# Where batches 1 to 7 and the later weights are prepared: all ahead, or between the pairs of batches 0 and 1

## What is computed

```python
xn = _layernorm(x, axis=-1)
x = x + _L0_attn_ref(xn, ...) + _L0_ffn_ref(xn, ...)
# _L0_attn_ref, 16 heads of 64
q = (x @ Wq + bq).reshape(b, s, H, L)
k = (x @ Wk + bk).reshape(b, s, H, L)
v = (x @ Wv + bv).reshape(b, s, H, L)
q = _apply_rope(q, cos, sin)
k = _apply_rope(k, cos, sin)
scores = jnp.where(causal, scores, -1000000000.0)
attn = jax.nn.softmax(scores, axis=-1)
return attended @ Wo + bo
# _L0_ffn_ref
x_scale = jnp.maximum(jnp.abs(x2).max() / 127.0, EPS)
x_int8 = jnp.clip(jnp.round(x2 / x_scale), -128, 127).astype(jnp.int8)
```

## Time and profile before

| | us |
| --- | --- |
| median of 3 executions | 1175.89 |
| lowest and highest | 1175.56 and 1179.27 |
| the profiled execution, as timed | 1179.43 |
| its span in the trace | 1177.6 |
| PE, DVE, ACT, POOL busy | 1029.2, 891.5, 690.7, 766.0 |
| span until VectorE's last row maximum | 100.4 |
| phases ahead of the pairs, until turn 0 on VectorE | 146.4 |
| second layer, after the last pair's `av` | 233 |

### The profile page before, as it was taken

How to read it: one execution, slowest core, us unless ns; L and a number is a source line. 1 busy time by engine, 2 the same in 40 slices (tenths; PEclk the granted TensorE clock), 3 DMA queues, 4 the chain that set the end, 5 groups by cost and what they waited for, 6 DMA issues and landing times.

```text
span 1177.6 us, 23657 instructions
## 1 busy us (share of the span) xinstructions
PE 1029.2 (87%) x7944; PEld 667.5 (57%) x7944; DVE 891.5 (76%) x1869; ACT 690.7 (59%) x1831; POOL 766.0 (65%) x949
## 2 busy tenths in 40 slices
PE   2005699999999999999999999999999965899988
PEld 1002265666766766666676676666667742454444
DVE  7695567777777777777777777777777637999996
ACT  1252276666666666666666666666667604766764
POOL 0081586777877687787777778677776515756662
PEclk9999899999999999999999999999999986999999
DMA  9303423233233223223323422332322000010001
GB/s 330 98 0 113 147 95 112 82 121 104 82 116 94 87 91 128 89 86 113 99 82 101 125 82 94 108 95 86 111 93 82 1 1 1 1 36 18 18 27 45
DMA packets 99693, 100.02 MB, mean 85 GB/s; under 512 B 12928, under 2 KB 94848, under 8 KB 99200
## 3 DMA queue, kind: packets, MB, share of 16 engines
q1 hardware_dynamic: 99584, 98.63, 25.8%
HBM read 56.64 MB, written 41.94 MB: 84 GB/s over the span
## 4 chain that ended last, share of the span: by engine, by line
PE 73%; DVE 17%; issue 3%; DMA 3%; ACT 1%; SPq 1%; DVEq 1%; POOL 0%; ACTq 0%; POOLq 0%
PE bank L1270 25%; PE bank L1358 13%; PE bank L1344 12%; PE bank L1373 7%; PE bank L1331 6%; PE bank L1332 5%; DVE arena L1181 3%; PE bank L1333 2%; DMA x_sb<-in_x 2%; DVE nm L1151 1%; PE bank L1520 1%; DVE wmax L952 1%; DVE arena L918 1%; DVE arena L1200 1%; DVE arena L1165 1%
## 5 line engine op out<-in xcount | busy, mean ns | idle before, releaser
L529 POOL TENSOR_SCALAR arena<-arena,rc 128x128 f32<-128x128 f32 (+3 forms) x512 | 274.9, 555 | 196.6 <-DVE rc L1031 196.6
L699 ACT ACTIVATE arena<-bank,nm 128x256 f32<-128x256 f32 (+3 forms) x512 | 268.0, 526 | 84.1 <-DVE nm L1023 75.2
L1023 DVE TENSOR_REDUCE nm<-bank 128x1 f32<-128x256 f32 (+3 forms) x512 | 230.0, 481 | 108.7 <-PE bank L1333 105.1
L1344 PE MATMUL bank<-ident,arena 128*128 128x128 f32 x1280 | 216.5, 277 | 4.8 <-DVE arena L1038 4.4
L1344 PEld LDWEIGHTS bank<-ident,arena 128*128 128x128 f32 x1280 | 143.7, 141 | 41.2 <-DVE arena L1038 20.3
L707 ACT ACTIVATE arena<-bank 128x512 f32<-128x512 f32 (+3 forms) x256 | 111.2, 434 | 80.0 <-PE bank L1344 79.8
L1332 PE MATMUL bank<-arena 128*128 128x256 f16 (+3 forms) x512 | 153.6, 300 | 0.0
L1358 PE MATMUL bank<-arena 128*64 128x512 f32 (+3 forms) x1024 | 151.9, 439 | 0.0
L1331 PE MATMUL bank<-arena 128*128 128x256 f16 (+3 forms) x512 | 147.8, 302 | 2.3 <-ACT arena L699 2.3
L1038 DVE COPY arena<-bank 128x512 f32<-128x512 f32 (+3 forms) x256 | 124.2, 485 | 23.8 <-PE bank L1344 19.9
L1358 PEld LDWEIGHTS bank<-arena 128*64 128x64 f32 x1024 | 67.8, 136 | 94.3 <-issue 71.3
(11 more groups left out here) (148 smaller groups left out, 2226.8 us busy)
## 6 DMA issues: line engine op xcount, KB each, us to landing
arena<-scr SPq DMA_DIRECT2D x320, 128.0 KB, 2.5
scr<-arena SPq DMA_DIRECT2D x256, 128.0 KB, 1.7
x_sb<-in_x SPq DMA_DIRECT2D x8, 512.0 KB, 6.4
arena<-in_weights SPq DMA_DIRECT2D x2, 2048.0 KB, 13.8
out<-x_sb SPq DMA_DIRECT2D x16, 256.0 KB, 2.2
xscr<-xsh SPq DMA_DIRECT2D x8, 256.0 KB, 2.3
xscr<-xsl SPq DMA_DIRECT2D x8, 256.0 KB, 2.2
xsh<-xscr SPq DMA_DIRECT2D x8, 256.0 KB, 3.2
```

The source lines that it names most:

```text
L529: last = pool.tensor_scalar(pr[slot][:, OFF[i]:OFF[i + 1]], pr[slot][:, OFF[i]:OFF[i + 1]], rc[:, slot, i:i + 1], 1.0, ALU.mult, ALU.mult)
L699: act.activation(pr[slot][:, OFF[i]:OFF[i + 1]], s_tile[i], ACT.Exp, bias=nm[:, slot, i:i + 1], accum_out=sm[:, slot, i:i + 1]).then_inc(e ...
L1023: dve.tensor_reduce(nm[:, slot, i:i + 1], s_tile[i], AX.X, ALU.max, negate=True).then_inc(max_done, 1)
L1344: last = pe.transpose(banks[5 + h][:, (i - j) * P:(i - j + 1) * P], pr[2 * par + h][:, OFF[i] + j * P:OFF[i] + (j + 1) * P], ident[:])
```

## The change

`wst`, `xn1` and the tables no longer have room of their own: they lie over the buffers of attention pieces and outputs that are not yet in use (`wst_qk` over `pr`, `tabraw` and `w8st` over `ptf`, `xn1` over `oth` and `otl`). The opening now does batch 0's rows and the query and key weights alone. GpSimd, not VectorE, writes the normal rows and the rotation tables; VectorE, not GpSimd, takes the low parts of the weights. VectorE's `early(n)` stands at the end of its turn n and holds the rest in portions; TensorE's `columns_of_rows(n, k)`, ScalarE's `columns_high` and VectorE's `columns_low` stand inside turns 1 to 7, and for turns 0 to 7 the copies of head 1's pieces 0 and 2 go from VectorE to ScalarE. The one reduction of the weights' maxima becomes four (query and key; values in turn -3; output weights in turn 3; second layer's in turn 10), and that of the rows' maxima comes in turn 6. The five first phases use two PSUM banks in turn (`o_bank`) instead of one, the first layer's steps of quantising batch 0 all come in turn 7, and the statistics write `mv3` without a copy.

```diff
+            load_rows(0)
+            for k in range(KT):
+                half = slice(k * C_V // KT, (k + 1) * C_V // KT)
+                sp.dma_start(wst_qk[:, half], weights_d[:, half]).then_inc(wqk_loaded, 16)
+            sp.dma_start(tabraw[:], tab_d).then_inc(tab_loaded, 16)
...
+            def normal_rows(b):
+
+                pool.wait_ge(roots_done, {0: 1, 1: 2, 2: 2, 3: 2}.get(b, 3))
+                after(pool, amax_done, b - 1)
+                after(pool, xt1_done, KT * (b - 1))
+                for c in range(NT):
+                    t = b * NT + c
+                    last = pool.tensor_scalar(xn1[b % 2][:, c, :], x_sb[:, t, :], mv3[:, t, 0:1], nw3[:, 0, t:t + 1],
+                                              ALU.subtract, ALU.mult)
+                last.then_inc(xn1_done, 1)
+
+            def weight_maxima(groups):
+
+                pool.wait_ge(wmax_done, groups.stop)
+                pool.partition_all_reduce(wall[:, groups], wmax[:, groups], P, bass.bass_isa.ReduceOp.absmax).then_inc(wall_done, 1)
+
+            normal_rows(0)
+            weight_maxima(slice(G_Q, G_V))
+            pool.wait_ge(setup_done, 1)
+            pool.wait_ge(tab_loaded, 16)
+            for g, by, dsts in ((G_Q, L ** -0.5, (cosq, sinq)), (G_K, 1.0, (cosk, sink))):
+                for a, dst in enumerate(dsts):
+                    last = pool.tensor_scalar(dst[:], tabraw[:, a], sc[:, g:g + 1], by, ALU.mult, ALU.mult)
+                last.then_inc(tab_done, 1)
...
+                if n == 1 - AHEAD + 1:
+                    weight_maxima(slice(G_V, G_O))
+                if 0 <= n < NB - 1:
+                    normal_rows(n + 1)
+                if n == 3:
+                    weight_maxima(slice(G_O, G_L))
+                if n == NB - 2:
+                    pool.wait_ge(xm_done, 1)
+                    pool.partition_all_reduce(xmax[:], xmax1[:], P, bass.bass_isa.ReduceOp.absmax).then_inc(xall_done, 1)
+                if n == 10:
+                    weight_maxima(slice(G_L, NG))
...
+            def later_weights(n):
+
+                if n == 2 - AHEAD:
+                    act.wait_ge(c_loaded, 16 * 4)
+                    act.activation(w8[:], w8st.rearrange("p (k c w) -> p k c w", k=KT, w=2)[:, :, :, 0], ACT.Copy).then_inc(w8_done, 1)
+                elif n == 3 - AHEAD:
+                    act.wait_ge(setup_done, 2)
+                    weights_high(G_V, wv_hi)
+                elif n == 4 - AHEAD:
+                    act.wait_ge(rows_mm, 1)
+                    for t in range(2):
+                        act.activation(fbow[:, t], ob[:, 0:D], ACT.Copy)
+                        last = act.activation(wsxw[:, t], ob[:, D:2 * D], ACT.Copy)
+                    last.then_inc(fb_done, 1)
+                elif n == 5:
+                    act.wait_ge(setup_done, 3)
+                    weights_high(G_O, wo_hi)
+                elif 12 <= n < 12 + NG - G_L:
+                    act.wait_ge(setup_done, 4)
+                    weights_high(G_L + n - 12, wr_hi)
...
+                if 1 <= n < NB:
+                    columns_high(n, 0)
+                if shared_copies(n):
+                    pt_whole(n, 0, 1)
...
+            row_sums(0)
+            inverse_roots(slice(0, 1), 0)
+            dve.wait_ge(wqk_loaded, 32)
+            weight_maximum(slice(G_Q, G_V))
             for k in range(KT):
-                dve.tensor_scalar(diag[:, k], ident[:], fbo[:, k:k + 1], None, ALU.mult)
-                last = dve.tensor_scalar(diag[:, KT + k], ident[:], vec[:, V_FS + k:V_FS + k + 1], None, ALU.mult)
-            last.then_inc(diag_done, 1)
-            dve.tensor_tensor(sc_vo[:], sc[:, G_V:G_V + 1], sc[:, G_O:G_O + 1], ALU.mult)
-            dve.scalar_tensor_tensor(out=sc_c[:], in0=sc[:, G_L:G_L + 1], scalar=D ** -0.5, in1=sc[:, G_R:G_R + 1],
-                                     op0=ALU.mult, op1=ALU.mult)
-            link(dset, dve.tensor_tensor(thr_c[:], inv[:, G_L:G_L + 1], inv[:, G_R:G_R + 1], ALU.mult))
-            dve.scalar_tensor_tensor(out=thr_c[:], in0=thr_c[:], scalar=D ** 0.5, in1=thr[:], op0=ALU.mult, op1=ALU.mult)
-            dve.tensor_scalar(sc_hr[:], sc[:, G_WR:G_WR + 1], 0.5, None, ALU.mult)
-            dve.tensor_scalar(sc_hv[:], sc[:, G_WV:G_WV + 1], 0.5, None, ALU.mult)
-            dve.tensor_scalar(omu[:], vec[:, V_MUR:V_MUR + 4], -1.0, 1.0, ALU.mult, ALU.add)
-            rows_of(1)
-            dve.wait_ge(amax_done, NB)
-            dve.tensor_reduce(xmax1[:], amax[:], AX.X, ALU.max).then_inc(xm_done, 1)
+                columns_low(0, k)
+            weight_scale(slice(G_Q, G_V), 0)
+            dve.wait_ge(b_loaded, 16 * 16)
+            for g in (G_Q, G_K):
+                dve.tensor_scalar(bcol[:, :, g - G_Q], bcol[:, :, g - G_Q], inv[:, g:g + 1], None, ALU.mult)
+            pairs_low(G_Q, 0)
+            pairs_low(G_Q, 1)
+
+            def early(n):
+
+                if n == -AHEAD:
+                    pairs_low(G_K, 0)
+                    pairs_low(G_K, 1)
+                    row_maximum(0)
+                elif n == 1 - AHEAD:
+                    dve.wait_ge(wv_loaded, 16)
+                    weight_maximum(slice(G_V, G_O))
+                    row_sums(1)
+                elif n == 2 - AHEAD:
+                    weight_scale(slice(G_V, G_O), 1)
+                    dve.wait_ge(consts, 6)
+                    bias_rows()
+                    dve.tensor_scalar(bvs[:], vec[:, V_BV:V_BV + NP], inv[:, G_V:G_V + 1], None, ALU.mult)
+                    row_sums(2)
+                elif n == 3 - AHEAD:
+                    weights_low(G_V, (wv_hi, 1), wv_lo)
+                    row_sums(3)
+                elif n == 4 - AHEAD:
+                    inverse_roots(slice(1, 4), 1)
+                elif n == 0:
+                    row_sums(4)
+                    row_sums(5)
+                elif n == 1:
+                    row_maximum(1)
+                    row_sums(6)
+                elif n == 2:
+                    row_sums(7)
+                    inverse_roots(slice(4, NB), 2)
+                    row_maximum(2)
+                elif n == 3:
+                    dve.wait_ge(wo_loaded, 16)
+                    weight_maximum(slice(G_O, G_L))
+                    row_maximum(3)
+                elif n == 4:
+                    weight_scale(slice(G_O, G_L), 2)
+                    dve.tensor_tensor(sc_vo[:], sc[:, G_V:G_V + 1], sc[:, G_O:G_O + 1], ALU.mult)
+                    row_maximum(4)
+                elif n == 5:
+                    row_maximum(5)
+                elif n == 6:
+                    weights_low(G_O, (wo_hi, 1), wo_lo)
+                    row_maximum(6)
+                    row_maximum(7)
+                    dve.wait_ge(amax_done, NB)
+                    dve.tensor_reduce(xmax1[:], amax[:], AX.X, ALU.max).then_inc(xm_done, 1)
+                elif n == 9:
+                    dve.wait_ge(wr_loaded, 16)
+                    weight_maximum(slice(G_L, NG))
+                elif n == 11:
+                    weight_scale(slice(G_L, NG), 3)
+                    dve.scalar_tensor_tensor(out=sc_c[:], in0=sc[:, G_L:G_L + 1], scalar=D ** -0.5, in1=sc[:, G_R:G_R + 1],
+                                             op0=ALU.mult, op1=ALU.mult)
+                    link(dset, dve.tensor_tensor(thr_c[:], inv[:, G_L:G_L + 1], inv[:, G_R:G_R + 1], ALU.mult))
+                    dve.scalar_tensor_tensor(out=thr_c[:], in0=thr_c[:], scalar=D ** 0.5, in1=thr[:], op0=ALU.mult, op1=ALU.mult)
+                    dve.tensor_scalar(sc_hr[:], sc[:, G_WR:G_WR + 1], 0.5, None, ALU.mult)
+                    dve.tensor_scalar(sc_hv[:], sc[:, G_WV:G_WV + 1], 0.5, None, ALU.mult)
+                    dve.tensor_scalar(omu[:], vec[:, V_MUR:V_MUR + 4], -1.0, 1.0, ALU.mult, ALU.add)
+                elif 13 <= n < 13 + NG - G_L:
+                    g = G_L + n - 13
+                    weights_low(g, (wr_hi, n - 12), wr_lo)
...
                 maxima(n + 1, 0, e, (1,))
                 out_low(n - 1)
                 maxima(n + 1, 0, e, (0, 2))
-                pt_whole(n, 0)
+                if not shared_copies(n):
+                    pt_whole(n, 0)
                 if tail and r % 4 == 0:
                     ffn_part(b - 1, r // 4)
                 maxima(n + 1, 0, e, (3,))
+                if 1 <= n < NB:
+                    columns_low(n, 0)
...
+                if n == NP - 1:
+                    input_scale()
+                    for step in range(4):
+                        quantise(0, step)
+                elif n >= NP and r >= NP - 4:
                     quantise(b, r - NP + 4)
+                early(n)
+                first_counts(n)
...
+            def columns_of_rows(b, k):
+
                 pe.wait_ge(xn1_done, b + 1)
-                after(pe, xtl_done, KT * (b - 1))
-                for k in range(KT):
-                    for c in range(NT):
```

(26 more changed lines are left out.)

351 lines of the change are left out of this document (197 added, 154 removed).

## The result

The changed kernel takes **1212.49 us** (median of 4 runs, 1211.29 to 1214.31) against 1176.79 for the kernel before (4 runs, 1175.56 to 1179.27): a ratio of 1.0293, 95% interval 1.0277 to 1.031. It is slower by 35.7 us. The forecast was 15.6 slower, 1191.5, and its range ended at 1210.

What follows compares the result with a forecast made beforehand. The prediction took VectorE's preparations to bound the opening and TensorE the rest up to 944 us. Terms -57.4 + 10 + 14 + 41 + 8 = +15.6 on 1175.9 gave 1191.5 us, range 1135 to 1210.

Steps and rivals of the forecast that it cites:

- term 1: Opening, before turn 0 on VectorE: the new order of preparations makes it shorter, -57.4 us.
- Term 2: Pairs 0 to 7: eight more transposes and head 1's copies behind ScalarE's exponentials make TensorE wait, +10 us.
- Term 3: Early turns: VectorE's portions (statistics, maxima, roots) exceed its 2.1 us free per turn, +14 us.
- Term 4: Turns 3, 6 and 10: GpSimd's code switches around reductions delay normalise, 14.75, 14.75 and 11.5, together +41 us.
- Term 5: Behind three TensorE stalls of over 10 us: the clock falls to 0.50, 2.75 us lost each, +8 us.
- A: Rival, GpSimd's reductions: the switch ahead costs nothing, only the one behind does; 1166 us, chance 0.22.
- B: Rival, pairs: switches do not hold them, the earlier 7.15 us being something else; 1126 us, chance 0.15.
- C: Rival, pairs: switches take longer under the pairs' own transfers, 10 us each; 1220 us, chance 0.08.

Runs made afterwards that it cites:

- 1, one factor: Changed kernel with GpSimd's rows multiplied by the root alone, the mean not subtracted (part of the computation left out): 1188.21 us, ratio 1.0097.
- 2, no switch in pairs: Changed kernel with the three partition reductions in turns 3, 6 and 10 replaced by plain copies (part of the computation left out): 1176.57 us, ratio 0.9993.
- 3, copies on VectorE: Changed kernel with head 1's pieces 0 and 2 copied by VectorE in all pairs, as before the change: 1198.95 us, ratio 1.0189.
- 4, sums in the opening: Changed kernel with the statistics of batches 2 to 7 and all roots taken by VectorE in the opening: 1207.49 us, ratio 1.0272.
- 10, all four: Changed kernel with reductions on TensorE and VectorE, sums in the opening, copies on VectorE, rows as product and sum: 1130.56 us against 1178.16 before.
- experiment 6: Kernel before with four added partition reductions on GpSimd, outputs unused (two in turn 20, one each in 30 and 40): 1212.33 us against 1177.06.
- experiment 9: Changed kernel with GpSimd's rows written as product and sum, same result: 1194.54 us, ratio 1.0142.

## Why the prediction was wrong in size

The direction held, and so did the way by which the switches and the copies reach TensorE; one price was wrong, and with it a whole loss was missing: the rows. The sum was 20 us short by the medians (35.7 against 15.6) and 16 by the traces (31.7). Like for like, at the end of pair 0 the forecast stood at -56.5 (term 1 and the 0.9 of pair 0) and the trace at -53.0; behind it the forecast added 72.1 and pairs 1 to 11 added 84.7. How these lengths are made up, in us, for pairs 1 to 11 of each profiled execution; the last column is an estimate, TensorE's busy time in each half microsecond times what was missing there to a clock of 1.00:

```
                          length  TensorE busy   idle   lost to the clock
before                    136.2      132.4        3.8       0.0
after                     220.9      155.4       65.5      16.0
1, one factor             204.2      152.2       52.0      13.6
2, no switch in pairs     187.6      155.2       32.3      15.9
3, copies on VectorE      209.8      151.4       58.4       9.9
4, sums in the opening    214.6      154.7       59.9      15.7
10, all four              152.4      143.5        8.9       1.4
```

Point by point:

- **Term 1, the opening, -57.4: it was -55.1 where I ended it and -53.0 at the end of pair 0.** Turn 0 starts on VectorE at 91.34 where I had 89.0. By the single steps: roots done at 9.38 (I had 9.3), maxima at 14.6 (14.3), then rows until 14.4 instead of 11.4 and a switch of 9.4 instead of 7.15, so the reduction at 23.8 instead of 18.6, and 9.1 back; key low parts done at 44.4 (38.3), GpSimd free after the second reduction at 66.9 (62.8). Of the 6 us of delay, 1 came back in the second switches (13.7 us with the reduction instead of 14.75) and 3.6 in the roots of three batches (85.54 to 91.18, 5.6 us instead of 9.2). VectorE's low parts beside GpSimd took 0.88 us each where 0.41 is their time alone: 7.05 us for the eight, 8.1 in my step. In the kernel after, first alone, then beside GpSimd:

```profile
25.55 3.26 DVE L1067 SCALAR_TENSOR_TENSOR wl<-arena,inv,wh 128x256 f16<-128x256 f32 x8 [0.39 <-ACT wh L730]
37.39 7.05 DVE L1067 SCALAR_TENSOR_TENSOR wl<-arena,inv,wh 128x256 f16<-128x256 f32 x8
```

- **Term 2, the copies, +10: about right, 13.5** in the changed kernel and 5.6 in the one with all four. The wait that I worked out as 1.5 us was 2.31. My own parts (12.16 + 0.9 + 1.5 - 0.18 - 0.36) make a turn of 14.0, not the 13.5 that I wrote; with it the term is 14. And 6.1 of the 11.1 us that the copies cost in pairs 1 to 11 came by the clock (estimate, table), which the term did not have.
- **Term 3, VectorE's portions, +14: too large for what was tested.** The statistics and roots cost 9.0 without rows and switches, and about 5 in the changed kernel, where the gain in pair 3 (8.1) is partly given back in pairs 2, 4 and 6. The portions of turns 4, 7 and 11 were in no experiment. It was right that turn 2 is the dear one, but I let a VectorE operation wait for one operation of GpSimd; here one waited 3.10 us, until 145.0, across two of GpSimd's (`rotate`, 142.46 to 144.97):

```profile
141.90 3.10 DVE L992 SCALAR_TENSOR_TENSOR nw<-nw 128x16 f32<-128x16 f32 x1
```

- **Term 4, the switches, +41: 36 by the medians, 33.3 of it in pairs 1 to 11** (experiment 2). The gaps came where they were foretold, between pairs 3 and 4, 6 and 7, 10 and 11, with TensorE's waits at 14.8 us in turns 3 and 6 against 14.75, and at 9.5 in turn 10 against 11.5. Turns 3 and 6 cost less than their waits because they were long anyway: with the reduction out, they still take 17.6 and 22.1 us, so a part of what I charged to the switch belongs to the rows and portions beside it.
- **Term 5, the clock, +8: about 16 in pairs 1 to 11** (estimate, table). Behind each of the three stalls there are 4 to 5.6 us at 0.50, as I had it. But the clock was at 0.50 also in pair 0 (94 to 101 us), pair 1 (115 to 118), pair 3 (146 to 155) and pair 5 (200 to 204), behind waits of up to 5.2 us, which I had not foreseen. Taking the three stalls out (experiment 2) gave back nothing of the 16; it fell where the small waits went: to 13.6 with fast rows, to 9.9 with the copies back on VectorE and to 1.4 with all four.
- **The step that failed** is in term 1 and term 4: "GpSimd writes the rows in 4 x 0.48", and "the new rows fill one" of its idle gaps. I took the price of a row from `normalise`, a product of 256 columns, for an operation that subtracts first. It costs 1.22. By shape from 100 to 245 us of the kernel after (busy us, mean ns):

```profile
L540 POOL TENSOR_SCALAR arena<-x_sb,mv,nw 128x256 f32<-128x256 f32 x28 | 35.3, 1275 | 0.0
L593 POOL TENSOR_SCALAR arena<-arena,rc 128x512 f32<-128x512 f32 x13 | 9.1, 699 | 0.0
```

  Seven turns with 4.87 instead of 1.92 are 20.7 us, and the idle time that should have taken the 1.92 (1.43 and 1.79 a turn) was far too short for 4.87. Undoing it gave 24 us (one factor) and 18 (same result, product first). Experiment 1 is nearly the kernel that I had costed, with four rows at 1.85: it lies 10.4 us above the kernel before (9.8 by the traces), within the range of the forecast and 5 from its 15.6. By the traces its opening gains 58.2 against my 56.5 and its pairs lose 68.1 against my 72.1. That these come so close is in part luck, since the clock was 5.6 too cheap (13.6 against 8) and the portions and switches too dear.

  The four effects taken out one at a time shorten pairs 1 to 11 by 16.6, 33.3, 11.1 and 6.3, 67.3 in sum. With all four out 16.2 us are left above the kernel before, of which the new transposes are some 6 (7 pairs of 0.9) and the rest stands in pairs 4, 7, 8 and 10. The two make 83.5 of the 84.7, so the four and what is left account for the loss.
- **The rivals.** A (the switch ahead is free) is refuted by the rows: 5.75 us or more, put to "issue", ahead of every reduction here and in experiment 6. B (the switches don't hold the pairs) is refuted by experiment 2. C, 10 us a switch in the pairs, is wrong there: they took 5.75 to 7.63, with 123 GB/s at most beside the way ahead (experiment 6) and at most 1 GB/s beside the way back. In the opening the first switches were longer, 9.4 and 9.1 us; over the seven kernels that have that reduction, the way ahead took 5.8 to 10.7 and the way back 7.9 to 14.1. That the transfers cause this isn't shown: the way back took 10.96 us at 354 GB/s in experiment 1, and 14.07 at 289 in experiment 9. The Trainium skill's figure for a first call to loaded code (GPSIMD Engine Reference, Instruction dispatch: about 6 us) agrees with the 5.75 to 6.31 ahead of a reduction in the pairs, and not with most of the opening's 5.8 to 10.7; the way back is a longer 6.8 to 7.6 in the pairs.

## What to carry to other kernels

Take the price of an operation from a row with the same operator and the same order of operators, not only the same engine, type and size; if there is none, bound it up to the dearest row of its kind, and ask what it does in each turn in which it stands. Work that leaves a bound opening is free in a steady loop only while each engine's added time stays under its idle time in one turn: here 0.4 us of reduction brought 14 us of switching and rows priced at 1.9 us took 4.9. Count what the lower clock costs over all waits of a stretch, small ones too: taking out the three long ones gave nothing of it back here. Collect the operations of a loaded kind on GpSimd into one place (a second one costs 0.4 us), or take them off it: a transpose, a row maximum and a small product did the same work, with a wait of 0.7 us in the opening.

## What the runs showed of the hardware

- GpSimd's `tensor_scalar` on 128x256 float32: product first, then a product or a sum, 0.46 to 0.55 us; subtraction first, then a product, 1.07 to 1.22 (one of 2.46); a single product or subtraction 0.92. A column in place of a constant costs about 0.1 at most.
- A partition reduction on GpSimd: 5.75 to 6.3 us ahead of it and 6.8 to 7.6 behind it in the pairs; 5.8 to 10.7 and 7.9 to 14.1 around the first one in the opening of seven kernels; the second of two in a row is free of both.
- A small chained operation of VectorE can wait long beside GpSimd: one step of the roots in turn 2 took 3.10 us, across two operations of GpSimd, its like 0.17.
- TensorE's clock was at 0.50 not only behind stalls of 14 us but behind one of 5.24 (pair 3), and in pair 1 behind waits of 0.87 and 2.31 us with work between them; in pair 2 it stayed at 1.00 behind one of 2.31. Stretches of the kernel after, pair 1, then pair 3, columns as above:

```profile
115.00:118.00 3.00, 3.00 (x17) 2.54 (x16) 2.23 (x5) 1.06 (x3) 0.74 (x3) 0.50 0.72 220
148.00:152.00 4.00, 1.54 (x6) 1.14 (x7) 1.94 (x4) 4.00 (x11) 1.25 (x2) 0.50 0.09 33
156.00:160.00 4.00, 4.00 (x26) 1.94 (x26) 3.59 (x10) 3.46 (x12) 3.44 (x6) 1.00 0.92 299
```
